# Summing both scan halves at once on GpSimd, into a buffer from which a DMA moves the backward half

## The reference

```
def _s5_scan(u, ...):
    lam_bar = jnp.exp(lam * dt)
    Bu = jnp.einsum('blh,ph->blp', u, B_bar)
    _, xf = associative_scan(_binop, (A, Bu), axis=1)
    _, xb = associative_scan(_binop, (A, Bu[:, ::-1]), axis=1)
    xs = jnp.concatenate([xf, xb[:, ::-1]], axis=-1)
    return 2.0 * jnp.real(jnp.einsum('blp,hp->blh', xs, Cc)) + D * u

def _s5_block(x, i, ...):
    fx = _layer_norm(x, ln1_g[i], ln1_b[i])
    h = _s5_scan(fx, ...)
    x = gelu(h) + fx
    fx2 = _layer_norm(x, ln2_g[i], ln2_b[i])
    return fx2 @ ff_enc[i].T @ ff_dec[i].T + fx2
```

## Time and profile before

| what | us |
|---|---|
| median of 3 runs | 11808.26 (11808.13 to 11818.87) |
| the profiled execution's own time | 11811.45 |
| its span, first to last instruction | 11809.7 |
| PE busy | 10767.5 (91%) |
| DVE busy | 7760.0 (66%) |
| ACT busy | 5016.4 (42%) |
| POOL busy | 2909.0 (25%) |
| POOL adds of `badd` (L1419), 496 of 64x512 | 849.8 |
| forward scans on DVE (L1387), 256 | 519.8 |
| backward scans on DVE (L1698), 256 | 341.2 |

### The profile page before, as it was taken

How to read it: one execution, slowest core, us unless ns; L and a number is a source line. 1 busy time by engine, 2 the same in 40 slices (tenths; PEclk the granted TensorE clock), 3 DMA queues, 4 the chain that set the end, 5 groups by cost and what they waited for, 6 DMA issues and landing times. The chain is left out here.

```text
span 11809.7 us, 159062 instructions
## 1 busy us (share of the span) xinstructions
PE 10767.5 (91%) x61986; PEld 7865.7 (67%) x61986; DVE 7760.0 (66%) x11075; ACT 5016.4 (42%) x7539; POOL 2909.0 (25%) x2580
## 2 busy tenths in 40 slices
PE   1999998988899998898989999889898999979988
PEld 1777765756677776575767777566576777747666
DVE  6555558878655556887855555687884555578787
ACT  0333333545633333454753333445474333345547
POOL 0111114243211112324221111332431111142333
PEclk6999998999999999998999999999899999989999
DMA  4333333444533333344443333434453222243445
GB/s 128 60 67 61 70 101 143 155 185 134 130 63 71 68 69 124 136 159 173 143 109 68 69 66 63 158 135 167 143 164 74 55 51 57 49 184 140 180 131 147
DMA packets 1183882, 1313.09 MB, mean 111 GB/s; under 512 B 825356, under 2 KB 1058204, under 8 KB 1080860
## 3 DMA queue, kind: packets, MB, share of 16 engines
q1 hardware_dynamic: 1183132, 1302.92, 38.5%
HBM read 787.50 MB, written 515.26 MB: 110 GB/s over the span
## 5 line engine op out<-in xcount | busy, mean ns | idle before, releaser
L969 POOL TENSOR_SCALAR xo<-xo 64x512 f32<-64x512 f32 x504 | 783.3, 1576 | 4878.8 <-DVE xo L1053 4878.8
L900 ACT ACTIVATE XF<-ps 128x340 f32<-128x340 f32 x1024 | 464.5, 454 | 3069.4 <-PE ps L757 3069.3
L1584 PE MATMUL ps<-fp,Dwr 128*128 128x512 f32 x6144 | 1483.6, 390 | 0.0
L1584 PEld LDWEIGHTS ps<-fp,Dwr 128*128 128x128 f32 x6144 | 1159.0, 189 | 245.7
L1026 DVE TENSOR_TENSOR Z<-ps,LW 128x340 f32<-128x340 f32 x1024 | 523.7, 511 | 1106.7 <-PE ps L766 1099.1
L1419 POOL TENSOR_TENSOR S<-tt 64x512 f32<-64x512 f32 x496 | 849.8, 1713 | 1055.4 <-DVE tt L1374 1033.9
L1190 PE MATMUL ps<-RS,Bc 128*128 128x128 f32 x4096 | 825.2, 329 | 288.0 <-DVE RS L1179 288.0
L1190 PEld LDWEIGHTS ps<-RS,Bc 128*128 128x128 f32 x4096 | 616.0, 209 | 657.8 <-DVE RS L1179 384.7
L1053 DVE TENSOR_TENSOR xo<-ps,raw 64x512 f32<-64x512 f32 x512 | 352.1, 688 | 995.1 <-PE ps L845 991.5
L1597 PE MATMUL ps<-XP,Cwr 128*128 128x512 f32 x3072 | 822.9, 404 | 172.5 <-DVE XP L1710 172.5
L803 PE MATMUL ps<-P,WP 128*106 128x512 f32 x3072 | 934.0, 439 | 0.0
(11 more groups left out here) (287 smaller groups left out, 21144.5 us busy)
## 6 DMA issues: line engine op xcount, KB each, us to landing
raw<-x SPq DMA_DIRECT2D x240, 640.0 KB, 8.3
fx_d<-fx SPq DMA_DIRECT2D x112, 1024.0 KB, 3.9
fl_d<-fp SPq DMA_DIRECT2D x112, 1024.0 KB, 5.0
fp<-fl_d SPq DMA_DIRECT2D x112, 1024.0 KB, 4.8
fx<-fx_d SPq DMA_DIRECT2D x112, 1024.0 KB, 5.0
x1h_d<-xo SPq DMA_DIRECT2D x256, 256.0 KB, 8.3
x1v_d<-xo SPq DMA_DIRECT2D x512, 128.0 KB, 5.1
xin<-x1v_d SPq DMA_DIRECT2D x64, 1024.0 KB, 4.8
```

The source lines that it names most:

```text
L969: ins = e.tensor_scalar(dst, src, 1.0, None, ALU.mult)
L1584: ins = e.matmul(ps[m % 2][:], Dwr[:, w, c:c + 128], fq[n % 2][x][:, s2, :], start=(s2 == 0 and w == 0 and x == 0), stop=False)
```

## The change

`Y` is two new buffers of 128 partitions x 2 x 512. For groups 0 to 14 POOL now makes two instructions of 128 partitions into `Y[g % 2]`, in place of four of 64 into `S`. The forward scan reads its input from `Y` and writes its result to `S`. The backward half is copied from `Y` to `S` by two DMAs of 64 partitions x 512 a group, issued by SP (`lane`). Stage B's scan waits for them (`lane_there`). Before POOL writes a `Y` again it waits for the DMAs and the scan of two groups earlier. Group 15 is summed as before.

```diff
+    Y = [at(f"Y{i}", [128, 2, 512]) for i in range(2)]
...
     def pa_sp(e, b, d):
         f = phase(b, d)
+
+        def lane(g):
+            k0 = 512 * g + 1
+            e.wait_ge(sem["badd"], NG * f + g + 1)
+            for j in range(2):
+                e.dma_start(S[j][64:128, k0 - 1:k0 + 511], Y[g % 2][64:128, j, :]).then_inc(sem[f"yl{g % 2}"], 16)
+
         for g in range(NG + 1):
+            if g >= 4:
+                lane(g - 4)
             if g + 2 < NG:
                 load_x(e, b, d, g + 2)
...
         for g in (NG - 4, NG - 3):
             fxs_there(e, f, g)
             fls_there(e, f, g)
+        for g in (NG - 3, NG - 2):
+            lane(g)
...
                 v = S[j][0:64, k0 + 1:k0 + 513]
-                e.tensor_tensor_scan(v, RR[0:64, d:d + 1].to_broadcast([64, 512]), v, S[j][0:64, k0:k0 + 1],
+                y = Y[g % 2][0:64, j, :] if g < NG - 1 else v
+                e.tensor_tensor_scan(v, RR[0:64, d:d + 1].to_broadcast([64, 512]), y, S[j][0:64, k0:k0 + 1],
                                      ALU.mult, ALU.add).then_inc(sem["scan"], 1)
...
+    def lane_there(e, f, g):
+        e.wait_ge(sem[f"yl{g % 2}"], 32 * ((7 if g % 2 else 8) * f + g // 2 + 1))
...
         for g in range(NG):
             e.wait_ge(sem["t"], M * f + 4 * g + 4)
-            if g < NG - 1:
-                badd(e, g, 0)
-            badd(e, g, 1).then_inc(sem["badd"], 1)
+            if g == NG - 1:
+                badd(e, g, 1).then_inc(sem["badd"], 1)
+            else:
+                if g >= 2:
+                    lane_there(e, f, g - 2)
+                    e.wait_ge(sem["scan"], 32 * f + 2 * (g - 2) + 2)
+                e.tensor_tensor(Y[g % 2][:, 0, :], tt[:, 0, :], tt[:, 1, :], ALU.add)
+                e.tensor_tensor(Y[g % 2][:, 1, :], tt[:, 2, :], tt[:, 3, :], ALU.subtract).then_inc(sem["badd"], 1)
             if g:
                 turn_pool(e, f, g - 1, slice(0, 64), 512 * g + 1, d)
...
         def scan(n):
             g = order[n]
             k0 = 512 * g + 1
+            if n:
+                lane_there(e, f, g)
```

More of the change, by code:

```diff
@@ L38 @@
     "xin0", "xin1", "kB", "kTi", "ctr", "sq0", "sq", "var", "sd", "rs", "bc", "nn", "f1", "f2", "bm", "t", "badd", "baddd",
-    "scan", "tn", "fxs0", "fxs1", "fls0", "fls1",
[1 row of a table added]
     "kD", "kC", "kTo", "fi_in0", "fi_in1", "fl_in0", "fl_in1", "fq0", "yd", "y", "gl", "x2", "xp0", "xp", "cc", "sr", "w", "tw", "va", "se", "tb",
```

## The result

The changed kernel takes **11499.23 us** (median of 4, 11494.95 to 11499.36) against 11808.19 (median of 4). The ratio is 0.9736, with a 95% interval of 0.9719 to 0.9753: 309 us less. The profiled execution took 11499.25 us, its span is 11497.5, so the spans differ by 312.2 us. The forecast was 11523 us, in a range of 11470 to 11620.

What follows compares the result with a forecast made beforehand. A loop between PE and DVE through `RS` was taken to bound stage A. Terms of 30.8 + 1.3 + 3.5 = 35.6 us a phase, by eight 285 us, gave 11523 us, range 11470 to 11620.

Steps and rivals of the forecast that it cites:

- What bounds: Stage A: a loop between PE and DVE through `RS` sets the group of 16.87 us; neither engine is full.
- The adds: POOL in stage A: a 128-partition add takes 1.3 us, between bounds of 1.26 and 2.52.
- Rival C: POOL's adds: a wide add costs twice a narrow one, so no change, 11808 us; chance 0.07.
- rival A: Stage A: wide add takes 1.55 us, `part` goes first, scans gain 1.2 us a group; 11583 us; chance 0.20.
- a wide add takes over 1.5 us: POOL in stage A: one of the signs that would show the forecast wrong; it took 1.3 us.
- The scans: DVE in stage A: two scans start after POOL's adds end and take 2.5 us, not 4.49: 2.0 us off each group.
- The clock: PE before L1190: wait falls to 0.7 us, half-clock groups vanish, 0.77 us a group gained.
- The sum: Whole kernel: a group takes 14.3 us; 35.6 us a phase, by eight 285 us, giving 11523 us.
- Head and tail: Start and end of stage A: shorter `part`s save 1.3 us a phase, an earlier last rotation 3.5 us.
- The DMAs and the waits: SP's 240 copies and POOL's added waits: cost 0, at most 10 us a phase if issue came through.
- Rival D: Copies out of `Y` land over 20.4 us after issue and POOL waits: slower, 11939 us at 24.4; chance 0.04.
- Rival B: Stage A: the `part` is freed too and PE's 13.4 us sets the group; 11435 us; chance 0.08.

Runs made afterwards that it cites:

- E1: The changed kernel, but with four adds of 64 partitions into the buffer instead of two of 128: 11806.04 us, ratio to before 0.9994.
- E4: The kernel before, with eight extra unread matmuls of 384 columns a group on PE where it waits for `RS`: 11783.09 us, ratio 0.9972.
- E7: The changed kernel, with every copy of the backward half issued a second time, into DRAM: 11497.89 us, ratio to before 0.9732.
- E5: The changed kernel, with the second rotation of a group moved up on DVE to right behind the first: 11391.45 us, ratio to before 0.9642.
- E2: The changed kernel, with two more wide adds on POOL a group, on a scratch tile, after the sums are reported: 11703.54 us, ratio 0.9905.
- E3: The changed kernel, with five memsets of 128x512 on POOL a group, after the sums are reported: 11501.92 us, ratio to before 0.9733.
- E8: E5's kernel, with DVE in stage B making `low` before `norm`: 11392.64 us, ratio to before 0.9642.

## Why the prediction was right

*What bounds.* Right. A loop from `RS` over PE to DVE and back to `RS` set the group, not PE's 91%: the windows fell when DVE's scans did, and PE's wait in front of L1190 fell with them, from 1.03 to 2.87 us to 0.77.

*The adds.* Right, and the value taken (1.3 us) was the right end of its bounds: 1.28. Rival C (twice the narrow one) is out, and so is the 1.55 us of rival A. The sign "a wide add takes over 1.5 us" must be read with care: the first wide add does, with a median of 1609 ns, but only because it waits for a `part`; its least is 1327.

*The scans.* 2.0 us off each group was forecast; 4.49 became 2.44, 2.05 us. The `part` was forecast to stay at 1.5 to 1.8 us and stayed at 1.70. E1 gives all of it back by the width of the adds alone. There was luck in it all the same. The order on which the forecast stood held by 0.13 to 0.16 us, less than the 0.25 us between the wide add taken and that of rival A, and the one group of a phase in which it did not hold has scans of 3.48 us. What the other order costs there is about 0.25 us (scans 1.04 longer, `part` 0.79 shorter), not the 0.8 us that rival A priced; no run has it in every group.

*The clock.* Right: with a wait of 0.77 us it is 1.00 in all windows. That a wait shorter than 1.03 us leaves it full was an estimate from the two waits of the earlier trace rows. Of the 2.83 us that a group gained, 2.05 are the scans', and 16.10 - 2.05 = 14.05 is the 14.04 measured. The rest, 0.78, is what was put down to the clock (0.77, from 16.87 - 16.10). No run shows that term by itself; what the trace of the kernel before shows is a mix of 31 groups at a clock of 1.00 with 16.08 to 16.12 us, 11 at 0.89 with 15.8 to 15.9, and 54 at 0.80 to 0.93 with 16.1 to 18.2. E4's groups bear the size out (58 at 1.00 with 16.08 to 16.15); moving the clock alone gave back 0.37 us a group, net of what the extra matmuls cost.

*The sum.* 14.3 us a group was too careful, 14.04 came out: 0.26 x 96 = 25 us, which is nearly the whole difference between the forecast's 285 and the 312 of the profiles. The two other terms missed by 8 us too much and 10 too little, and that they cancel is luck. The lower end, 14.1, had been worked out and then left for a margin that the trace did not ask for.

*Head and tail.* The tail was under-sized and the head over-sized. At the end of the stage 3.5 us were forecast. In the fifth phase the last rotation began 22.96 us after `RS` of group 15 (7739.91 - 7716.95) and now begins 19.02 after it (7543.14 - 7524.12), 3.94 less; over all phases the time behind the steady windows is 38 us less, 4.8 a phase. The adds of group 14 are what DVE waits for, before and now. They start 1.25 us earlier, as forecast, but last 4.30 us (7538.74 to 7543.04), not the 5.1 of the term, and 6.98 before. The rest is the clock, which the term left out: in five of the eight phases the stretch from `RS` of group 15 on had a clock of 0.73 or 0.74 and took 36.8 to 37.0 us, and now takes 31.7 at 0.84; in the other three (0.79 or 0.80) it took 35.6 to 35.8.

The head lost 2.5 us in eight phases rather than 10, and there too the term missed the clock. The `part`s are as short as forecast: DVE is busy 23.8 us in that stretch for 25.2. At the same clock the stretch is 1.1 us shorter, 34.11 for 35.2 at 1.00 and 35.7 for 36.85 at 0.95. But three phases had 1.00 there before, and one has it now, while two have fallen to 0.91 and take 37.3.

*The DMAs and the waits.* Right at nothing: they land in 5.5 us (6.8 at the most), where 20.4 were reckoned to be available and 19.8 are. The issue was mis-sized: 0.32 us was taken for it, from a row of 128 partitions, and it takes 1.09 (median), 2.5 for the two. SP had the time. E7 doubles the copies for nothing. Rival D (slower) had no support.

*Rival B* (PE as the bound, group 13.4) did not come with the change, because the `part` stayed held, as was argued. It came with E5, which frees that `part`, at 13.04 us.

## What to carry to other kernels

When one shape of a DVE instruction takes 0.7 us in one place and 1.7 in another, look at what GpSimd is doing there, and ask which of the two reads what: here adds (E2) brought the scans to 2050 ns, and memsets (E3) left them at 1267. An add of 64 partitions was no cheaper hold here than one of 128 (1259 and 1276 ns at the least). Where that is so, sum both halves in one instruction, even if a DMA must then carry one of them to its place. But first try to move GpSimd's work beside DVE instructions that read PSUM: in E5 an add took 1.30 us beside two of them, and they took 1.28. That was a one-line move, here worth 230 us alone, three quarters of what the buffer and 240 copies give, and together they give 420. Before either, see that the held instruction is on the loop that sets the time: in E8 it was made half as long and nothing followed.

## What the runs showed of the hardware

An add on GpSimd of 512 elements in each partition takes 1276 ns for 128 partitions and 1259 for 64, at the least. Memsets on GpSimd (525 ns for 128x512, 534 at the most) pass beside DVE's scans (1267 ns in E3, 1266 in the change) with no effect that the trace shows on either. A GpSimd add whose two inputs and output are one tile of zeros takes 1030 ns at the least; which of these makes it shorter is not shown. And SP needs longer to issue a copy out of `Y` (a median of 1.09 us) than one of stage A's loads and stores of 128 partitions, which take 0.32 us each. By source, in the change, and for E7's second copy, from the same place into DRAM:

```profile
L1162 SPq DMA_DIRECT2D S<-Y x240: 461/1092/1542, 1743.3 to 11031.9; - x120
...
L1164 SPq DMA_DIRECT2D again_d<-Y x240: 446/704/1402, 1741.2 to 11030.9; - x120
```

So it is not only that both ends lie in SBUF: the copy into DRAM takes up to 1.40 us too. Other issues of the kernel take more than 0.32 us as well: those of `x1v_d<-xo`, also 128 KB, have a median of 0.67. Why is open. It costs nothing here: with twice as many, E7 is 1.3 us from the change. What two such issues a group cost in a kernel whose DMA queue is full, no run shows.
